# Splitting the expert weights two blocks per body, with the high parts stored to DRAM and loaded again in the last body

## What is computed

```python
x = x + attention(layernorm(x), ctx)            # per batch: q, k, v, softmax, out
logits = x_n @ Wg + bg;  gates = top2(softmax(logits / 5))
h = gelu(x_n @ W1[e] + b1[e]);  y_e = h @ W2[e] + b2[e]
x = x + sum over e of gates[e] * y_e            # x_n is the second layernorm
```

## Time and profile before

| | |
|---|---|
| median of 3 runs | 833.87 us (827.43 to 835.49) |
| the profiled execution | 829.04 us, of which the trace's span is 827.3 us |
| TensorE busy | 767.5 us (93% of the span) |
| VectorE, ScalarE, GpSimd busy | 629.3, 452.4, 394.7 us |
| chain that ended last | PE 73%, DVE 10%, DMA 6%, issue 4% |
| mean DMA rate | 149 GB/s |

### The profile page before, as it was taken

The page is one execution under the profiler, slowest core; times in us unless marked ns, Lnnn a source line. Parts: engine busy times, 40 slices in busy tenths (PEclk is TensorE's granted clock), DMA queues, the critical chain, the costliest instruction groups (busy, mean ns, idle before and its releaser), DMA issues.

```text
span 827.3 us, 16330 instructions
## 1 busy us (share of the span) xinstructions
PE 767.5 (93%) x4698; PEld 459.5 (56%) x4698; DVE 629.3 (76%) x1131; ACT 452.4 (55%) x667; POOL 394.7 (48%) x358
## 2 busy tenths in 40 slices
PE   8599999999999999999999978678999989999995
PEld 4343434544434444444444423247989879998894
DVE  6786678798788798798778787866786887776674
ACT  2166676775775775776765655453345434444441
POOL 6506142446446456455425347654344455443444
PEclk9689999999999999999999979869999999999999
DMA  5766566567667667657467535263454456444441
GB/s 190 232 172 195 129 206 196 154 201 230 172 197 231 170 197 237 161 174 237 134 185 250 160 78 166 85 232 73 77 91 79 73 120 116 74 77 70 73 74 12
DMA packets 90285, 123.66 MB, mean 149 GB/s; under 512 B 15081, under 2 KB 52937, under 8 KB 89817
## 3 DMA queue, kind: packets, MB, share of 16 engines
q1 hardware_dynamic: 75832, 104.74, 43.2%
q0 software_dynamic: 13296, 17.09, 11.9%
q10 hardware_dynamic: 1072, 0.79, 0.3%
HBM read 64.96 MB, written 57.75 MB: 148 GB/s over the span
## 4 chain that ended last, share of the span: by engine, by line
PE 73%; DVE 10%; DMA 6%; issue 4%; ACT 2%; POOL 2%; SPq 0%; DVEq 0%; POOLq 0%; ACTq 0%
PE ps_pv L1483 14%; PE ring L1470 11%; PE ring L1625 9%; PE ring L1607 9%; PE ring L1457 7%; PE ps_x L1511 6%; DMA out<-y_sb,xs 5%; PE ps_x L1529 4%; DVE negm L1012 4%; PE ps_x L1501 3%; PE ps_x L1521 3%; PE ring L1616 3%; PE ps_x L1538 2%; PE ps_pv L1598 1%; ACT probs L944 1%
## 5 line engine op out<-in xcount | busy, mean ns | idle before, releaser
L1012 DVE TENSOR_REDUCE negm<-ring 128x2 f32<-128x1024 f32 x256 | 310.3, 1222 | 76.2 <-PE ring L1457 74.2
L944 ACT ACTIVATE probs<-ring 128x1024 f32<-128x1024 f32 x256 | 260.6, 1024 | 98.4 <-PE ring L1470 98.2
L845 POOL DMA_INDIRECT out<-y_sb,xs x71 | 110.3, 1554 | 138.3 <-DMA out<-y_sb,xs 82.6
L1483 PE MATMUL ps_pv<-probs,v_aug 128*32 128x512 f32 x1024 | 141.4, 625 | 5.3 <-ACT probs L944 5.2
L1470 PE MATMUL ring<-q_st,k_st 64*128 64x512 f32 x512 | 128.9, 503 | 6.5 <-DVE negm L1012 6.5
L1457 PE MATMUL ring<-k_st,q_st 64*128 64x512 f32 x512 | 110.7, 432 | 11.3 <-ACT probs L944 5.2
L1470 PEld LDWEIGHTS ring<-q_st,k_st 64*128 64x128 f32 x512 | 48.6, 188 | 107.7 <-issue 77.2
L973 ACT CAST xsT_hi<-ps_pv 128x256 fp32r<-128x256 f32 x71 | 26.4, 372 | 134.3 <-PE ps_pv L1598 134.3
L716 POOL DMA_INDIRECT xs_dram<-xg,rows x64 | 65.2, 1019 | 56.1 <-DVEq L1180 25.8
L1625 PE MATMUL ring<-w_hi,hT_hi 128*128 x284 | 85.7, 302 | 2.5 <-POOL w_lo L743 2.4
L1625 PE MATMUL ring<-w_lo,hT_hi 128*128 x284 | 80.3, 283 | 0.0
(11 more groups left out here) (194 smaller groups left out, 1236.6 us busy)
## 6 DMA issues: line engine op xcount, KB each, us to landing
k_st<-k_dram SPq DMA_DIRECT2D x64, 192.0 KB
q_st<-q_dram SPq DMA_DIRECT2D x64, 192.0 KB
xs<-xs_dram SPq DMA_DIRECT2D x71, 132.5 KB, 2.2
k_dram<-qk_hi SPq DMA_DIRECT2D x32, 256.0 KB, 2.4
q_dram<-qk_hi SPq DMA_DIRECT2D x32, 256.0 KB, 2.8
o_dram<-oT SPq DMA_DIRECT2D x32, 256.0 KB, 2.7
x_all<-in_x SPq DMA_DIRECT2D x8, 512.0 KB, 4.8
k_dram<-qk_lo SPq DMA_DIRECT2D x16, 256.0 KB, 2.3
```

The costliest lines, as they stand in the source:

```text
L845: pool.indirect_dma_start(out=out, out_offset=bass.IndirectOffsetOnAxis(ap=xs[j % AHEAD][:, TOKEN:TOKEN + 1].bitcast(I32), axis=0), in_=y_ ...
L944: nc.scalar.activation(probs[:, kt, 2 * jp:2 * jp + 2, :], ring[PLACE["ST", u, p] % RINGS][:], ACT.Exp).then_inc(exp_done, 1)
L1012: nc.vector.tensor_reduce(negm[:, v % 2, :, jp, kt], ring[PLACE["MX", v, p] % RINGS][:], AX.X, ALU.max, negate=True).then_inc(max_free, 1)
L1483: mm = nc.tensor.matmul(ps_pv[2 * DH * j:2 * DH * (j + 1), :], v_aug[:, kt, HPG * g + j, :], probs[:, kt, j, :], start=(kt == 0), stop=(kt ...
```

## The change

Bodies 1 to 6 each split two blocks: W1 of experts 0 to 6 and W2 of experts 0 to 4, twelve in all (`STAGED`). ScalarE rounds a block into `stage`, which is the memory of `w1_sb[7]`, in slots (1, 2) and (3, 2); GpSimd makes the low part from it where it is to stay; SP stores the stage to DRAM. In the last body SP loads seven `w1_hi` and, with ScalarE's queue for one, five `w2_hi`, 512 KB each, where attention is done with their memory. W1 of expert 7 is loaded raw in the last body only; it and W2 of experts 5, 6 and 7 are split there by ScalarE (high) and VectorE (low). GpSimd splits nothing after body 6. The slots of the last body's other work are moved, and `load_w2(7)` and `load_b2` stand at other places in SP's order.

```diff
-LAST_POST = {(1, 1): "OP0", (1, 3): "OP1", (1, 4): "OP2", (1, 5): "OP3",
-             (2, 5): "XG0", (2, 7): "XG1", (3, 1): "LG", (3, 6): "PX"}
+LAST_POST = {(1, 3): "OP0", (1, 4): "OP1", (1, 5): "OP2", (1, 6): "OP3",
+             (2, 5): "XG0", (2, 6): "XG1", (2, 7): "LG", (3, 5): "PX"}
-LAST_LN2 = {(1, 4): "stats0", (1, 6): "stats1", (1, 7): "sums"}
+LAST_LN2 = {(1, 5): "stats0", (1, 7): "stats1", (2, 0): "sums"}
+STAGED = {1: ((1, 0), (1, 6)), 2: ((1, 1), (2, 0)), 3: ((1, 2), (2, 1)), 4: ((1, 3), (2, 2)), 5: ((1, 4), (2, 3)), 6: ((1, 5), (2, 4))}
+STAGE_SLOTS = {(1, 2): 0, (3, 2): 1}
-LAST_TABLES = {(2, 0): "tiles", (2, 2): "past", (2, 4): "rows"}
+LAST_TABLES = {(2, 1): "tiles", (2, 2): "past", (2, 3): "rows"}
+LAST_HIGH = {(2, 1): (2, 5), (2, 4): (1, 7), (3, 6): (2, 6)}
+LAST_LOW = {(2, 4): (2, 5), (2, 6): (1, 7), (3, 7): (2, 6)}
...
+            def store_stage(i, n):
+                layer, e = STAGED[i][n]
+                sp.wait_ge(staged, stage_no(i, n) + 1)
+                sp.dma_start((w1_dram if layer == 1 else w2_dram)[e].rearrange("p c h -> p (c h)"),
+                             stage.rearrange("p c h -> p (c h)")).then_inc(stage_stored, 16)
+            def load_w2_hi(e):
+                sp.wait_ge(st_full, NP * (G - NG + e % NG + 1))
+                sp.dma_start(w2_hi[:, e].bitcast(F32), w2_dram[e]).then_inc(w2_hi_in, 16)
...
-            def high_w1(e):
-                pool.wait_ge(w1_in, 16 * E)
...
-                nc.gpsimd.tensor_copy(w1_hi[:, e], w1_sb[:, e]).then_inc(w1_hi_done, 1)
+            def low_staged(i, n):
+                layer, e = STAGED[i][n]
+                pool.wait_ge(staged, stage_no(i, n) + 1)
+                nc.gpsimd.tensor_tensor(low_part(layer, e), weights(layer, e), stage, ALU.subtract).then_inc(stage_low, 1)
...
+            def high_staged(i, n):
...
+                if k > 0:
+                    act.wait_ge(stage_stored, 16 * k)
+                    act.wait_ge(stage_low, k)
+                nc.scalar.copy(stage.bitcast(F32R), weights(layer, e)).then_inc(staged, 1)
...
+            act.wait_ge(st_full, NP * G)
+            act.dma_start(w2_hi[:, 3].bitcast(F32), w2_dram[3]).then_inc(w2_hi_in, 16)
             take_o(G - 1)
...
-                        pe.wait_ge(w2_split, E)
+                        pe.wait_ge(w2_hi_in, 16 * (E - 3))
+                        pe.wait_ge(low_done, 4)
```

More of the change, by code:

```diff
@@ L410, in sum_of, with weights, high_part, low_part @@
             return x_of(b) if b < B - 1 else xg[:, :, 0:D]
+        stage = w1_sb[:, E - 1]
+        def weights(layer, e):
+            return w1_sb[:, e] if layer == 1 else x_of(e).rearrange("p t d -> p (t d)").rearrange("p (c h) -> p c h", c=DC)
+        def high_part(layer, e):
+            return w1_hi[:, e] if layer == 1 else w2_hi[:, e].rearrange("p c d -> p (c d)").rearrange("p (c h) -> p c h", c=DC)
+        def low_part(layer, e):
+            return w1_lo[:, e] if layer == 1 else w2_lo[:, e].rearrange("p c d -> p (c d)").rearrange("p (c h) -> p c h", c=DC)
+        def stage_no(i, n):
+            return 2 * (i - 1) + n
         block = stack.enter_context(nc.Block())
@@ L547, in body @@
                     load_stack(i, 3)
+                    if not more:
+                        load_w2(E - 1)
                     put_recip(i - 1, 1)
@@ L554, in body @@
                     store_parts("Q", i + 1, 0)
+                if not more:
+                    for e in (0, 1, 2):
+                        load_w1_hi(e)
                 put_max(i, 2)
@@ L557, in body @@
                     load_stack(i + 1, 0)
+                else:
+                    for e in (3, 4):
+                        load_w1_hi(e)
                 put_o(NG * i)
@@ L561, in body @@
                     store_parts("K", i + 1, 1)
-                if not more:
-                    load_w2(E - 1)
-                    load_b2()
+                else:
+                    for e in (0, NG):
+                        load_w2_hi(e)
+                    sp.wait_ge(stage_low, ALL_STAGED)
+                    load_w1(E - 1)
+                if i in STAGED:
+                    store_stage(i, 0)
                 put_max(i, 3)
@@ L567, in body @@
                     load_stack(i + 1, 1)
+                else:
+                    for e in (5, 6):
+                        load_w1_hi(e)
                 put_o(NG * i + 1)
+                if not more:
+                    load_w2_hi(1)
                 if i > 0:
@@ L572, in body @@
                 fetch_o(i, 0)
-                if more:
+                if i < B - 2:
                     load_w1(i)
-                if i == B - 2:
-                    load_w1(E - 1)
+                if i == 0:
+                    load_w1(E - 2)
                 if more:
@@ L579, in body @@
                     load_stack(i + 1, 2)
+                else:
+                    load_b2()
                 put_o(NG * i + 2)
+                if not more:
+                    load_w2_hi(2)
+                if i in STAGED:
+                    store_stage(i, 1)
                 if i > 0:
@@ L801, in body @@
                     split("K", i + 1, 1)
-                if i == B - 1:
-                    for e in range(E):
-                        high_w1(e)
+                if i in STAGED:
+                    low_staged(i, 0)
                 if i > 1:
                     scatter(i - 2, NP * (NG * i + 1) + SCATTER if i < B - 1 else None)
-                if i == B - 1:
-                    for e in range(2):
-                        low_w1(e)
                 if i > 0:
                     ln2(i - 1)
-                if i == B - 1:
-                    for e in range(2, E - 2):
-                        low_w1(e)
                 if i + 2 < B:
@@ L1631, in _ @@
             turn_x(0)
-            pe.wait_ge(w1_split, E)
+            pe.wait_ge(w1_hi_in, 16 * (E - 1))
+            pe.wait_ge(stage_low, ALL_STAGED)
+            pe.wait_ge(low_done, 2)
             hidden(0, e[0])
```

121 lines of the change are left out of this document (53 added, 68 removed).

## The result

The changed kernel takes 825.62 us (median of 10 runs, 823.71 to 828.13), the kernel before 833.87 (10 runs, 827.43 to 835.9): a ratio of 0.9911, 95% interval 0.9889 to 0.9933. The prediction was 819 us. So the gain is 8.2 us (0.9%) where 14.9 were forecast, and by the 1% of the prediction it is no longer "faster". The two profiled executions are nearer to each other than the medians: 828.13 and 829.04 us, spans 826.4 and 827.3. The 829.04 us is the execution profiled ahead of the prediction; it is not one of the ten beside the changed kernel.

What follows compares the result with a forecast made beforehand. Bodies 1 to 6 were taken as bound by TensorE, the last body's first three units by DVE. Terms summed to -11.6 us, 817.4 us from the profiled 829.04, with the median placed at 819 us; range 811 to 828.

Steps and rivals of the forecast that it cites:

- bodies 1 to 6: Bodies bound by TensorE: ACT's copy at (3,2) delays the next exponential 0.3 us per body, +1.8 us in six.
- last body, first unit: POOL's high parts go, five VectorE operations fall to 0.19 us each: -3.3 us, bounds 1.5 and 4.2.
- second unit: Last body: OP0 moves from slot (1,1) to (1,3), giving PE score work before its wait: -2.2 us.
- third unit, with the clock: Last body: tables end earlier, ACT gets XG0 5.5 us sooner, and 1.0 us for PE's clock: -6.5 us.
- fourth unit: Last body: ACT, taken as the bound, makes W2's high part of expert 6: +1.0 us, bounds 0 and 4.
- start of the tiles: POOL's two low parts of W2 go, with the first output's 2.44 us wait: -2.4 us, bounds 1 and 4.
- the passage on POOL in bodies 1 to 6: Two subtractions per body, 2.3 us each, fit POOL's 29 us to spare; paced scatter catches up: cost 0, bounds 0 and 3.
- ACT's copies: Two 1.04 us copies per body in bodies 1 to 6: cost 0 at (1,2), 0.3 us at (3,2).
- The rival with copies at their full length: ACT's copies are not hidden in bodies 1 to 6 and cost 12.5 us: 830 to 833 us, chance 0.07.
- The rival of the blocked VectorE: POOL's twelve subtractions block VectorE in bodies 1 to 6, 2.1 us each: +12 us, 843 us, chance 0.05.
- more than the sum: Last body: PE's clock stays up and the fourth unit gains as well: -18 us, 812 us, chance 0.12.
- the loads take the freed time: Last body becomes bound by DMA, some 5 to 6 us of the gain go: -6 us, 825 us, chance 0.15.

Runs made afterwards that it cites:

- series A: The run of the result: changed kernel beside the kernel before, 825.62 against 833.87 us, ratio 0.9911.
- series B: Changed kernel run a second time, beside an edit of no effect and two combinations of edits: 816.62 us, before 829.78, ratio 0.9838.
- series D: Changed kernel 830.34 us, before 832.84; beside them no stores 829.3, subtraction behind the scatter 821.7, kernel before with filler ahead of the scatter 842.58.
- null edit: Changed kernel with one more semaphore increment on SP behind the last body, which nobody waits for: 817.12 us, ratio 0.9838.
- later-reciprocal kernel of the last series: Changed kernel with POOL's first subtraction behind the scatter and VectorE's reciprocal of the last denominators later: 817.26 us, ratio 0.9815.
- series C: Changed kernel run a third time, beside a later reciprocal, OP0 back at (1,1), and later reciprocal with copy at (3,7): 830.09 us, before 834.09, ratio 0.9965.
- later reciprocal: Changed kernel with VectorE's reciprocal of the last denominators moved behind the first tile's first loop step: 827.89 us, ratio 0.9932.
- four edits: Changed kernel, each with one edit, run without it: subtraction behind the scatter 817.35 us, copy at (3,7) 818.37, no stores 816.52, two W2 loads later 819.18.

## Why the prediction was right or wrong

The terms of the sum, against series A (with pauses) and B (without), from the starts of `take_o` and of the first `output` in each profile:

| term, us | forecast | series A | series B |
|---|---|---|---|
| up to the last unit of body 0 | 0 | +1.2 | +0.5 |
| bodies 1 to 6 | +1.8 | +10.4 | +2.4 |
| last body, first unit | -3.3 | -4.8 | -4.2 |
| second unit | -2.2 | -1.6 | -2.8 |
| third unit, with the clock | -6.5 | -2.5 | -5.2 |
| fourth unit | +1.0 | -2.4 | -1.8 |
| start of the tiles | -2.4 | +2.0 | -0.3 |
| the tiles themselves | 0 | -3.2 | -2.4 |
| sum | -11.6 | -0.9 | -13.8 |

**The step that failed** is the passage on POOL in bodies 1 to 6: "The first stands in front of the scatter, whose eight DMAs are paced by score slots and catch up. [...] Cost 0, bounds 0 and 3". They do catch up, and catching up is the cost: the paced DMAs become a burst, and on three of six occasions the burst brought a common pause of about 1.2 us per body. Beside the changed kernel in series D, the subtraction behind the scatter took the pause away and 8.6 us with it; without the stores the pause stayed. Counted in series A against B, the third units of bodies 2 to 6 hold 5.5 us of the 7.9 us more. The rest lies in the fourth and first units, where PE's granted clock fell for a moment. That the pause brings these moments too is not shown: body 1, which has no scatter, has one in series A (16.28 us in its fourth unit), and so has the null edit of series B (16.42 us), a kernel without pauses. Around the end of body 4 the mean is 0.93 and 0.64 in two stretches of series A, and 1.00 in series B.

```profile
358.00:362.00 4.00, 3.99 (x31) 2.37 (x29) 2.92 (x5) 2.08 (x3) 0.00 (x0) 0.93 0.39 131
362.00:366.00 4.00, 4.00 (x19) 2.17 (x21) 2.13 (x7) 2.60 (x6) 0.73 (x1) 0.64 0.26 82
```

**The frame** was the second fault. The sum of the terms is 11.6 us, but 819 us lies 14.9 us under the median of the kernel before, since it starts from the profiled execution (829.04 us) and not from the median (833.87 us). No term stands for the other 3.3 us; put on the median, the sum gives 822.3 us. Two figures of the paragraph on DMAs are off as well and change nothing: by the terms of the sum the last body would last 59 us, not 57, and one MB at the estimated 300 to 335 GB/s of a full share is some 3 us of the engines' time, not 5.

**ACT's copies** were sized right. In series B the fourth units of bodies 1 to 4 take 15.07 to 15.09 us against 14.86 to 14.88 before, 0.2 us each where 0.3 was forecast, and their second units are within 0.05 us of before, so the copy at (1,2) costs nothing. With the copy at (3,7) the fourth units are back at 14.86, but the first unit behind them takes 16.3 us at full clock instead of 15.8 (bodies 3 and 5 of that kernel), so the slot with the longer idle time was the worse one by 0.3 us. The rival with copies at their full length is out.

**The rival of the blocked VectorE** did not occur: bodies 1 to 6 have no VectorE operation of 2 us beside the subtractions, and DVE's busy time in a body is 51.02 us where it was 51.00. Beside POOL's split of the next batch's k such holding is there in both kernels (`row_k` 1.0 us instead of 0.19), and where it hits two of these operations, as in body 5 of series B, the second unit takes 16.4 instead of 15.8 us.

**The last body** came out at 58.7 and 55.9 us, forecast 59. First unit: the routing operations take 0.19 us (0.73 to 1.02 in the earlier trace rows), and the unit gained 4.8 us in series A and 4.2 in B, at and above the upper bound of 4.2. Its clock rose from a mean of 0.73 to 1.00 and 0.96, for which the sum had no term in this unit. The rival "more than the sum" had named that, and it is in part what series B shows. The third unit goes with the clock: 13.89 us at 1.00 in series B, 16.66 at 0.81 in A. The fourth unit is the plainest case of that, 15.12 us at a mean of 0.50 and 11.55 us at 1.00, with the same instructions in the unit; the later-reciprocal kernel of the last series, and the changed kernel of series B:

```profile
526.12:541.24 15.12, 12.55 (x60) 2.98 (x60) 6.72 (x28) 8.58 (x10) 3.04 (x3) 0.50 0.85 294
```

```profile
522.88:534.43 11.55, 7.25 (x60) 2.06 (x60) 6.70 (x28) 8.39 (x10) 2.55 (x2) 1.00 0.92 320
```

The changed kernel itself took 15.13 us there in series C, also at 0.50. Most of that came back at the start of the tiles, 13.3 us in series C and 15.8 in B.

The third unit's step holds. ACT's wait for `row_tab`, 7.76 us in the earlier trace rows, is gone; POOL's `xg` is what XG0 waits for. The load of W2 for expert 6, for which I had added 1.0 us, made ACT wait 0.63 us in series B and not at all in A. The fourth unit's own step failed: "ACT bounds this unit" was to make it 1.0 us longer, but ACT had been busy for 7.63 of 13 us, and with the copy in it (8.4 us busy) the unit came out 2.4 and 1.8 us shorter, at a clock of 0.97 and 1.00 against 0.89. How much of that is the clock is open.

**The start of the tiles** was another miss: the forecast took the wait of the earlier trace rows away and asked what is late next only of PE's order, not of the DMAs. The rival "the loads take the freed time" has its place here and not in the last body: with twelve high parts to fetch, b1 was issued at 543.3 us instead of 539.4, and the last denominators lie behind it. The Trainium skill says that descriptors of one queue start in order on an engine ("DMA: Bandwidth & Descriptors", section "Two DMAs through the same engine are not ordered"); with 9.0 us for a transfer of 8 KB issued behind b1's 2 MB, and at most 3.4 us before, the trace agrees. It costs the forecast 4.4 us there in series A and 2.1 in B, and no more than the runs can tell at the end, as the later reciprocal showed. The last three rows of the table trade with each other: from the start of the fourth unit to the end of the span it is 290.3 to 291.7 us in the four profiles of the changed kernel, 295.2 before. Why the tiles themselves took 2.4 to 3.2 us less than before is not settled.

The range was held (811 to 828) and the sign was right, the size was not: 0.81 for "over 1% faster" left too little room for a step that was priced at nothing because its engine has time to spare.

## What to carry to other kernels

Work that is put ahead of paced DMAs on an idle engine turns the pacing into a burst: cost the burst, or put the work behind them, and look at what it holds there. With the subtraction behind the scatter this kernel had ratios of 0.981 and 0.986, on an occasion of either kind; the changed kernel had 0.984 on one without pauses and 0.991, 0.9965 and 0.996 on three with them. Before crediting an edit, run the unedited kernel in the same series: four edits here seemed to win 6 to 9 us that were the occasion's.

## What the runs showed of the hardware

A pause of PE, ACT and VectorE at once, 1.2 to 2.5 us, behind five to eight indirect DMAs that POOL issued 0.30 us apart (1.27 us from start to start), in every body from 2 on, on three of six occasions. With the later five of the eight DMAs 0.7 to 0.9 us apart no trace shows one, in series D neither. Nor does every burst bring one: the profile of the kernel before has one of eight without it. What makes an occasion one with pauses was not found: one chip had both kinds. What stands still is not shown either; matmuls and DMAs of POOL that had been released ran on, and the starts that came late were those that wait for another engine, some marked as released from elsewhere (3.91 us on ACT in the last rows of the kernel with the subtraction behind).
